# Local attention scores as two-head products two units deep, remote scores by key block, and token transfers that wait for the group in front

## The reference

```
attention: 16 heads, 4 key heads; q = 32 semantic + 32 rotated features, v = 64 features
  keys: 14 means over blocks of 64 tokens (the first 896 tokens) + the last 128 tokens one by one = 142 keys
  scores = (q_sem.k_sem + q_geo.k_geo)/sqrt(32) * exp(logit_scale[h]);  hidden where k_pos > pos
  out = softmax(scores) v, times Wo
  (a token below 63 sees no key: its 142 weights are all equal)
experts: softmax router over 16, the best 4 per token, weights renormed;
  out = sum over the 4 of weight * down_e(silu(gate_e x) * up_e x), inner width 224
```

## Time and profile before

| | us |
|---|---|
| median of the 3 timed runs | 413.79 (413.33 to 415.93) |
| the profiled execution's own time | 414.26 |
| span of its instructions | 412.5 |
| PE busy / DVE busy / ACT busy / POOL busy | 367.9 / 263.2 / 185.9 / 233.3 |
| front (until the first local score) | 0 to 63.7 |
| local stage | 63.7 to 131.2 |
| remote stage | 131.2 to 206.8 |
| expert loop and its tail | 206.8 to 412.5 |

### The profile page before, as it was taken

The page is one execution under the profiler, slowest core; times in us unless marked ns, Lnnn a source line. Parts: engine busy times, 40 slices in busy tenths (PEclk is TensorE's granted clock), DMA queues, the critical chain, the costliest instruction groups (busy, mean ns, idle before and its releaser), DMA issues.

```text
span 412.5 us, 8607 instructions
## 1 busy us (share of the span) xinstructions
PE 367.9 (89%) x2263; PEld 309.1 (75%) x2264; DVE 263.2 (64%) x837; ACT 185.9 (45%) x537; POOL 233.3 (57%) x205
## 2 busy tenths in 40 slices
PE   0599995968998999799899999999999999999991
PEld 0483474756885677577678899999999999999881
DVE  4889244897924799999857755555555555555540
ACT  1541236543521265225537655555555555555550
POOL 3501556566555435994605666566666666666664
PEclk9999997897999999999779999999999999999996
DMA  7991222212114963068545666676667667667544
GB/s 246 357 316 46 78 78 78 78 64 92 52 66 143 319 208 110 21 195 222 152 141 101 104 107 116 103 110 110 111 106 112 114 106 112 112 106 112 78 52 51
DMA packets 49016, 51.41 MB, mean 125 GB/s; under 512 B 5472, under 2 KB 46048, under 8 KB 48992
## 3 DMA queue, kind: packets, MB, share of 16 engines
q0 software_dynamic: 14640, 19.34, 28.3%
q1 hardware_dynamic: 34352, 31.78, 27.2%
HBM read 29.67 MB, written 21.43 MB: 124 GB/s over the span
## 4 chain that ended last, share of the span: by engine, by line
PE 71%; DVE 14%; issue 7%; ACT 3%; DMA 2%; SPq 1%; POOLq 1%; another core or an unknown queue 0%; DVEq 0%; ACTq 0%
PE bank L1292 59%; PE bank L1654 4%; PE bank L1678 4%; DMA x_all<-in_L_attn_x 1%; ACT lex L760 1%; DVE q L1073 1%; DVE q L1070 1%; ACT x_all L692 1%; PE bank L1445 1%; PE bank L1416 1%; DMA out_rows<-y,idx 1%; DVE l L1097 1%; DVE pr L1213 1%; DVE xr L1241 1%; DVE pr L1233 1%
## 5 line engine op out<-in xcount | busy, mean ns | idle before, releaser
L670 POOL DMA_INDIRECT out_rows<-y,idx x79 | 122.9, 1556 | 81.8 <-ACT y L854 63.2
L648 POOL DMA_INDIRECT xn_by_expert<-x_all,slot_i x64 | 64.9, 1014 | 20.4 <-issue 15.7
L1272 DVE SCALAR_TENSOR_TENSOR act<-bank,xg,sg 128x224 f32<-128x224 f32 x79 | 35.6, 450 | 51.5 <-ACT sg L841 50.7
L1292 PE MATMUL bank<-wgu_hi,xh 128*128 x158 | 65.2, 413 | 0.5 <-issue 0.2
L1292 PE MATMUL bank<-wgu_lo,xh 128*128 x158 | 58.5, 370 | 0.0
L1292 PE MATMUL bank<-wgu_hi,xl 128*128 x158 | 57.9, 366 | 0.0
L841 ACT ACTIVATE sg<-bank 128x224 f32<-128x224 f32 x79 | 28.3, 358 | 60.6 <-PE bank L1292 59.7
L1264 DVE TENSOR_TENSOR xl<-bank,xh 128x256 fp32r<-128x256 f32 x79 | 33.5, 424 | 29.4 <-ACT xh L834 29.1
L1292 PE MATMUL bank<-wdn_hi,ah 112*128 x158 | 51.3, 324 | 0.5 <-issue 0.4
L1292 PE MATMUL bank<-wdn_hi,al 112*128 x158 | 44.4, 281 | 0.0
L1292 PE MATMUL bank<-wdn_lo,ah 112*128 x158 | 44.2, 280 | 0.0
(11 more groups left out here) (238 smaller groups left out, 766.1 us busy)
## 6 DMA issues: line engine op xcount, KB each, us to landing
xg<-xn_by_expert SPq DMA_DIRECT2D x79, 129.0 KB, 2.5
wgu<-in_L_ffn_gate_proj SPq DMA_DIRECT2D x16, 224.0 KB, 5.4
wgu<-in_L_ffn_up_proj SPq DMA_DIRECT2D x16, 224.0 KB, 5.8
wdn<-in_L_ffn_down_proj SPq DMA_DIRECT2D x16, 224.0 KB, 6.2
x_all<-in_L_attn_x SPq DMA_DIRECT2D x8, 256.0 KB, 4.8
xr<-in_L_attn_x SPq DMA_DIRECT2D x14, 128.0 KB, 4.6
out_rows<-xr SPq DMA_DIRECT2D x14, 128.0 KB
out_rows<-y,idx POOLq DMA_INDIRECT x79
```

The costliest lines, as they stand in the source:

```text
L648: gp.indirect_dma_start(xs_d, bass.IndirectOffsetOnAxis(slot_i[:, z, r:r + 1], 0), x_all[:, z, :], None).then_inc(xs_in[q], DMA)
L670: gp.indirect_dma_start(out_rows, bass.IndirectOffsetOnAxis(idx[r % RING][:, 0:1], 0), ysb[r % 4][:, :], None, compute_op=ALU.add).then_in ...
L1272: nc.vector.scalar_tensor_tensor(av[t.par][:, :], bank[2 + t.par][:, I:2 * I], xg[t.slot][:, D + 1:D + 2], sg[t.par][:, :], ALU.mult, ALU. ...
L1292: return nc.tensor.matmul(o, lhsT, rhs, start=start, stop=stop)
```

## The change

- **Local scores.** Keys are stored twice per key head with every second head's rows zero (`keep_rep` makes two activations each, scaled by `sscale`). `l_score` makes for each pair of heads one product of 64 rows and 284 columns per feature kind, after a bfloat16 product (identity times mask) that puts the mask into PSUM: 2 + 2 + 2 products into 2 banks. Units alternate between banks (1, 2) and (3, 5), and PE runs two units ahead. DVE's `l_largest` takes minus the maximum straight from PSUM in two reduces; ACT takes the exponentials from PSUM. The copy with the mask is gone.
- **Values.** `fold_values(g)` is one product of 58 weight columns and 512 columns per key head; ACT copies it to `folded`, SP writes it to HBM in the new order (12 DMAs) and reads `vw` back (3 DMAs, semaphore `vw_in`).
- **Columns block by block** (key outer, head inner). Pair t uses 2t+2 blocks, so 32(t+1) columns in scores, exponentials, sums and turns; one turned chunk instead of two for t below 4. The mask of the last two blocks is a bfloat16 product of 32 columns; DVE masks by itself only at t = 0. The maximum is taken from PSUM, and the subtraction reads PSUM and `smax`. PE writes the `bd_g` and `fold_queries` products with four columns together and a step of 16.
- **Token transfers.** Each indirect DMA waits only for the one at the same place p of the group in front.
- **Moved.** `plan_tasks`, `weights(2)`, `weights(3)`, diagonals of `bd_s` go ahead of the local rope, `bound_tasks` behind it; splits: 3 low parts on DVE (was 4), POOL 10 (was 9); experts 13 to 15 are loaded behind the first eight task loads, which the last two stores now part in 4 + 4; their splits come at steps 5 to 7 and 6 to 8, expert 12's high part at step -1.

```diff
-LATE = ((4, 5), (6, 7), (8, 9), (10, 11), (12,), (13, 14, 15))
+LATE = ((4, 5), (6, 7), (8, 9), (10, 11, 12), (13,), (14,), (15,))
-ON_DVE = 4
+ON_DVE = 3
@@ SP
             load_residual(0)
+            for g in range(HKV):
+                sp.wait_ge(fold_kept, g + 1)
+                for m in range(2):
+                    sp.dma_start(vw_rows[:, :, 2 * g + m, :], folded[g % 2][0:FOLD - NB, m, :]).then_inc(folded_out[g % 2], DMA)
+                sp.dma_start(even_rows[:, 2 * g:2 * g + 2, :], folded[g % 2][FOLD - NB:FOLD, :, :]).then_inc(folded_out[g % 2], DMA)
+            for q in range(2):
+                sp.wait_ge(folded_out[q], 3 * HKV // 2 * DMA)
...
+            for i in range(REMOTE - 3):
                 store_sum(i)
                 load_residual(i + 2)
+                if i == 2:
+                    for p in range(GT):
+                        sp.wait_ge(xs_in[p], K * GROUPS * DMA)
+                    load_late(3)
...
+            for j in range(RING // 2, RING):
+                load_task(j, j)
+            for n in range(4, len(LATE)):
+                load_late(n)
@@ POOL
-                    for z in range(q * GT, (q + 1) * GT):
-                        gp.indirect_dma_start(...).then_inc(xs_in[q], DMA)
-                    gp.wait_ge(xs_in[q], (r + 1) * GT * DMA)
+                    for p in range(GT):
+                        z = q * GT + p
+                        if r or q:
+                            gp.wait_ge(xs_in[p], (r * GROUPS + q) * DMA)
+                        gp.indirect_dma_start(...).then_inc(xs_in[p], DMA)
@@ DVE
+                for m in range(2):
+                    last = nc.vector.tensor_reduce(lneg[q][:, 2 * m:2 * m + 2], bank[L_BANKS[q][m]][:, 0:2 * NKEY].rearrange("p (h k) -> p h k", h=2), axis=AX.X, op=ALU.max, negate=True)
...
+                link(nc.vector.tensor_reduce(smax[u][:, :], by_head(scores, t), axis=AX.X, op=ALU.max))
                 if not t.first:
                     dve.wait_ge(c_pt[u], t.count(0))
+                nc.vector.tensor_tensor(by_key(pr[u], t), by_key(scores, t), over_heads(smax[u][:, :], t), ALU.subtract).then_inc(c_d[u], 1)
@@ PE
+                if n >= 2:
+                    pe.wait_ge(l_ex, n - 1)
+                for m in range(2):
+                    mm(out[m], ident_b[:, :], hide_lb[:, :, :].rearrange("p h k -> p (h k)"), True, False)
+                for m, own in enumerate(halves):
+                    mm(out[m], qrT[u][own, g, :], rep_g[own, g, u, :, :].rearrange("p s k -> p (s k)"), False, False)
+                for m, own in enumerate(halves):
+                    last = mm(out[m], qsT[u][own, g, :], rep_s[own, g, u, :, :].rearrange("p s k -> p (s k)"), False, True)
...
+            l_score(0)
+            l_score(1)
+            for n in range(UNITS):
+                l_turn(n)
+                if n + 2 < UNITS:
+                    l_score(n + 2)
+                if n:
+                    l_value(n - 1)
+                beside(n)
+                if n == UNITS - 2:
+                    turn_values(0)
```

More of the change, by code:

```diff
@@ L168, in build @@
         asem = wat.take("asem", [P, NB, DC, HK])
-        vw = wat.take("vw", [HALF + 1, NB, 2, D])
-        bd_g = wat.take("bd_g", [P, NB, HKV, G, NBLK])
-        pr = [wat.take(f"pr{u}", [P, HK + 1]) for u in range(NB)]
+        vw = wat.take("vw", [P, NB, 2, D])
+        bd_g = wat.take("bd_g", [P, NB, HKV, NBLK, G])
+        pr = [wat.take(f"pr{u}", [P, HK]) for u in range(NB)]
         smax = [wat.take(f"smax{u}", [P, H]) for u in range(NB)]
@@ L181, in build @@
         qrT = [wl.take(f"qrT{u}", [P, HKV, P]) for u in range(NB)]
-        prT = [wl.take(f"prT{u}", [HALF + 1, 2, P]) for u in range(NB)]
+        prT = [wl.take(f"prT{u}", [P, 2, P]) for u in range(NB)]
         lpT0 = wl.take("lpT0", [P, G, P])
+        ident_b = wl.take("ident_b", [P, P], BF16)
+        hide_b = wl.take("hide_b", [P, 2, H], BF16)
         wb = r_loop[1]
@@ L431, in first, with keys, cols, chunks @@
                 return self.counts is None and self.off == 0
+            @property
+            def keys(self):
+                return 2 * self.off + 2
+            @property
+            def cols(self):
+                return self.keys * H
+            @property
+            def chunks(self):
+                return [(at, min(P, self.cols - at)) for at in range(0, self.cols, P)]
             @property
@@ L552, in load_residual @@
                         sp.wait_ge(c_stored[u], i * DMA)
-                    sp.dma_start(residual(u, i)[:, :], rows(x_rows, u * TB + i)).then_inc(xr_in[i % 2][u], DMA)
+                    sp.dma_start(residual(u, i)[:, :], rows(x_rows, u * TB + i)).then_inc(lx_in if i == REMOTE - 1 else xr_in[i % 2][u], DMA)
             def store_sum(i):
@@ L574, in _ @@
             load_late(2)
[L575 to L582, removed]
+            load_residual(REMOTE - 1)
+            for i in range(REMOTE - 3):
                 store_sum(i)
                 load_residual(i + 2)
+                if i == 2:
+                    for p in range(GT):
+                        sp.wait_ge(xs_in[p], K * GROUPS * DMA)
+                    load_late(3)
+            store_sum(REMOTE - 3)
             def load_task(j, s):
@@ L592, in _ @@
                 sp.wait_ge(c_s[u], REMOTE)
-            for j in range(RING):
+            for j in range(RING // 2):
                 load_task(j, j)
@@ L837, in step @@
                         p_keep(u, Pair(0, REMOTE - 1))
+                    for k in HEAD:
+                        split_late(k)
                 t = j + 1
@@ L994, in _ @@
             weights(1)
+            weights(2)
             iota_p = const(ca, CA, "iota_p")
@@ L1584, in attend @@
                 o = attended_bank(u, t)[:, 0:D]
-                mm(o, prT[u][0:HALF, 0, :], vw[0:HALF, u, 0, :], True, False)
-                mm(o, prT[u][:, 1, :], vw[:, u, 1, :], False, True).then_inc(c_o[u], 1)
+                parts = [(prT[u][0:rest, n, :], vw[0:rest, u, n, :]) for n, (at, rest) in enumerate(t.chunks)]
+                if t.first:
+                    parts.append((even, vw[0:EVEN_AT + EVENS, u, 1, :]))
+                for n, (turned_p, values) in enumerate(parts):
+                    last = mm(o, turned_p, values, n == 0, n == len(parts) - 1)
+                last.then_inc(c_o[u], 1)
             def attention_pe(t):
```

404 lines of the change are left out of this document (202 added, 202 removed).

## The result

The changed kernel took 467.84 us (median of four, 464.26 to 468.85) against 414.86 for the kernel before on the same chip: a ratio of 1.126, interval 1.118 to 1.134. The forecast was 389, the range 380 to 401. It is slower by 53 us instead of faster by 25.

The account below looks back on a forecast made before the run. PE was taken to lead the local stage, PE and DVE (swollen beside POOL) the remote stage, PE alone the expert loop. Sum: 414.3 - 16.3 (local) - 12.2 (remote) + 3.5 (loop head) = 389.3, so 389 us; range 380 to 401.

Parts of the forecast that it names:

- the one on token transfers: POOL's transfers: about 5.6 us a group instead of 6.91, end at 130 to 138 us, no term in the sum.
- the slower one: Rival, expert loop's head: experts 13 to 15 get only crumbs beside the scatters; 425 us at 35 GB/s, chance 0.03.
- Start of the local stage: Front: stage starts 0.4 us later for the starts product; work moved ahead of it costs nothing.
- Local stage: First score to second `q_project`: 50.8 us instead of 67.5, of which PE's work 46.8; gain 16.3 with the later start.
- A score unit: Local scores: 1.2 us a unit, 0.96 with row halves overlapping plus 0.24 for masks; 2.2 if not.
- The waits: Local stage: 1.6 us at the start and 0.8 of small waits, beside 1.6 for slow clock.
- `vw`: Round trip through HBM in the local stage: back at 35 to 40 us, needed at 42; cover 2 to 7, cost 0.
- Remote stage: Remote pairs: 63.4 us instead of 75.6, with 5.4 less PE work through fewer columns; gain 12.2.
- PE's stalls: Remote stage: 3 us of stalls left of 9.8, between 0 and 9.8, as the subtraction reads PSUM.
- The rival of strided PSUM columns: `bd_g` products and query folds: strided writes slow PE, losing 3 us and 2.7 us; 395 us, chance 0.05.
- Head of the expert loop: Start of the expert loop: costs 3.5 us, as experts 13 to 15 are issued ahead of task 8's load.
- Task 8: Head of the expert loop: its load comes 1 to 8 us late behind the expert loads; 3.5 taken.

Follow-up runs that it names:

- run 9: Changed kernel, not altered, run again as control in another session: 395.61 us, ratio 0.959 to the kernel before.
- run 2: Kernel before, with each token transfer waiting only for the one at its place in the group in front: 410.26 us, ratio 0.993.
- run 11: Changed kernel with one wait a group, remote pairs 1 to 6 taking all 224 columns again (block by block undone): 400.53 us.
- Run 10: Changed kernel with one wait a group, experts 13 to 15 loaded beside remote pair 5, ahead of the task loads: 390.78 us, ratio 0.946.
- first eight runs: Variants of the changed kernel and one of the kernel before (transfer waits, memsets, expert loads), two sessions without late signals: from 391.75 to 415.31 us.
- run 13: Changed kernel, not altered, once more in a further session: 469.12 us.
- run 14: Changed kernel with one single pause in POOL's row of transfers, after the eighth group: 461.35 us.
- run 17: Changed kernel with the wait for the whole group of transfers put back: 418.20 us.
- run 18: Changed kernel with one wait a group and experts 13 to 15 loaded early, in a session with late signals: 460.14 us.
- run 4: Changed kernel with single waits kept and five short memsets on POOL behind each group (7.4 us a group): 407.08 us.
- the best version: Changed kernel with one wait a group and experts 13 to 15 loaded early: 390.78 us without late signals, 460 us with them.
- run 1: Changed kernel with token transfers again waiting for all four of their group: 415.31 us, ratio 1.005.

## Why the prediction was wrong

**The step that failed** is the one on token transfers: "That is no term by itself". The reckoning of the transfers was right (5.3 us a group against 5.6, last one at 127.1 against 130 to 138). What it took away were the group waits, with their pauses and their empty queue, and it asked only who waits for the transfers, not whom they hold up. What the runs showed in its place: PE's signals, and PE itself, were held up until the row of transfers was over, and the local stage started 68.6 us late. The trace of before had a sign. `l` L1097 lists "remote 0.6" in the earlier trace rows, and the waits of ACT hold three more, of which one is this (the kernel before, all engines in order of time):

```profile
85.56 0.66 PE L1445 MATMUL bank<-const_k,lex 128*128 128x128 f32 x4 [0.23 <-issue]
...
86.68 0.97 POOL L648 DMA_INDIRECT xn_by_expert<-x_all,slot_i  x1 [0.30 <-issue]
...
88.57 0.58 ACT L767 COPY lpT<-bank 128x512 f32<-128x512 f32 x1 [1.71 <-remote]
...
89.64 0.19 POOL L645 COPY x_all<-weight 128x4 f32<-128x4 f32 x1 [1.99 <-DMA xn_by_expert<-x_all,slot_i]
```

PE's four turns ended at 86.2, ACT saw it at 88.6, 0.9 us after POOL's last transfer of the group (86.68 + 0.97) and inside its pause. The other three end in a pause of POOL, or as it begins (at 81.78, 102.96 and 109.62). The traces of the sessions without late signals have no such row. A wait of 2 us that nothing in a one-core program ends is a sign that something outside the sum holds signals up. No rival had it either: the slower one was another mechanism at 425.

**The other steps** can be read in the changed kernel's trace without late signals (run 9, span 393.0 us; the forecast as a span is 389.3 - 1.8 = 387.5). Its windows, then PE at the start of the stage:

```profile
65.30:117.20 51.90, 50.62 (x306) 37.06 (x307) 26.90 (x79) 26.28 (x92) 40.28 (x48) 1.00 0.34 118
117.20:179.50 62.30, 60.04 (x336) 42.68 (x334) 53.18 (x125) 27.62 (x63) 41.69 (x29) 1.00 0.57 169
```
```profile
65.32 0.41 PE L1342 MATMUL bank<-hide_lb,ident_b 128*128 128x284 bf16 x2 [0.78 <-ACT qrT L801]
65.66 0.75 PE L1342 MATMUL bank<-rep_g,qrT 64*128 64x284 f32 x4
66.25 0.65 PE L1342 MATMUL bank<-rep_s,qsT 64*128 64x284 f32 x4
66.82 0.42 PE L1342 MATMUL bank<-hide_lb,ident_b 128*128 128x284 bf16 x2
```

- Start of the local stage: 65.3, forecast 64.1 (63.7 + 0.4). 1.2 late: the front was not free. Some 0.7 of it is there at the first copy of `qsT` already (57.45, against 56.71 in run 2, whose front is that of before).
- Local stage: 51.9, forecast 50.8. PE's work is 50.6, not 46.8. A score unit is 1.50 us start to start (66.82 - 65.32), not 1.2: the masks take 0.34 instead of 0.24, the four float32 products 1.16, nearer to full overlap of the halves (0.96) than to none (1.92). That is +2.4 in eight units; the other 1.4 was not taken apart. The waits are 1.3 us and the clock 1.00, where 4.0 had been given for both. Two errors that partly cancel.
- `vw`: SP issues its last loads at 99.6 to 100.9, and PE uses them first at 109.7, without a wait. That is 8.8 us for the landing and the cover. The trace has no landing time for them; with the 2.5 to 5 us of the prediction the cover would be 4 to 6 (an estimate), forecast 2 to 7. 0 was right.
- Remote stage: 62.3 to its last product ahead of the tasks' turns, forecast 63.4. PE's stalls in it are 2.3 (forecast 3.0). The subtraction of 224 columns now takes 0.392 us, beside POOL too, against 1.233 in the earlier trace rows. The product with `srec`, two SBUF inputs, takes 1.145 us for 160 columns beside a split of POOL's (164.2 to 165.4 us), 0.313 for the same 160 columns right behind it, and 0.36 for 192 columns in a gap between two splits (174.3). So far the trace agrees with the Trainium skill ("SBUF — State Buffer", Who interferes with whom), by which two SBUF inputs are blocked and one is not.
- The rival of strided PSUM columns: the four products with `bd_g` of one batch (eight records) take 1.08 us in run 11 at 56 columns, against 0.99 in the earlier trace rows. That is 0.09 a batch, not a slowdown that counts. It doesn't clear the writing itself: the same four take 1.04 us with 8 columns in run 9, so at 56 most of a slower write could still be hidden, as the prediction had said. The sentence in the Trainium skill ("SBUF — State Buffer", the paragraph on cachelines) that any non-contiguous PSUM access pattern slows matmuls significantly is not borne out for these products, in rows of four columns.
- One reading in the prediction is wrong without effect: 0.19 us is the cost of one record of a 224-column product, not of the product (0.76 for four records, which are two products, in the earlier trace rows). The saving was reckoned from the 0.76.
- Head of the expert loop: from the last product ahead of the turns of tasks 0 and 1 to the end 213.5 us (393.0 - 179.5), before 205.7 (412.5 - 206.8), so +7.8 where 3.5 had been forecast. This is the term that was mis-sized.

PE's waits from 200 to 222 us show its parts:

```profile
PE bank L1714 <- DMA xg<-xn_by_expert: 3.9, 1, 3.9
PE bank L1342 <- DVE wdn_lo L1178: 2.5, 1, 2.5
```

Task 8 is 3.9 us late, near the estimate. The 2.5 us are PE waiting for DVE's low part of the last expert. The prediction named these splits, but as waiting for the same bytes as task 8, and put no price of their own on them. Some 1 more are tasks 0 and 1, which wait 1.02 and 0.51 for their rows (before, PE waited 0.57 at that place, for DVE). Run 10, with the loads early, has tasks 8 and 9 in step (200.12 and 202.50, 2.38 apart) and keeps the 2.5. So it isn't the bytes: there ACT has made the last high part by 207.2, and DVE works without a gap until its last low part is done at 210.7. What is left as a cause, and was not tested, is the splits' move to steps 6 to 8 (was 2, 4, 6), for the first gate product of the rolled loop waits for all sixteen low parts, and the kernel before does not stand there.

Together: 1.2 + 1.1 - 1.1 + 4.3 = 5.5, which is 393.0 - 387.5. Without late signals the forecast of 389 stands against 395.6, inside its range, the head of the loop being most of what is missing. In the session of the measurement 67.4 us of later start (132.7 - 65.3) come on top, and 1.1, 2.7 and 1.6 in the stages behind: 72.8 together, the whole difference of the spans (465.8 - 393.0).

## What to carry to other kernels

A wait that goes takes a pause, and a limit on what is under way, with it. Before counting it as waste, look for waits whose releaser the profile doesn't know, and at whether they end in such pauses; in a one-core program a row that says "remote" is a finding, not noise. And when variants disagree with the original, run the original beside them in the same session first: the first eight runs here were read against a time from another one. The same goes within a pair of runs: compare the stretch ahead of the edit's first effect before giving the edit what lies behind it.

## What the runs showed of the hardware

- While GpSimd issued indirect DMAs without a gap (0.97 us each, 0.3 between them), semaphore signals of TensorE reached ScalarE and VectorE up to 52 us after the matmul had ended in the measured trace (58 us in run 13, `vloc`: 63.0 to 120.9), in three of the seven sessions; signals of ScalarE to TensorE were not late (0.14 us). TensorE's own instructions stalled too: eight turns took 4.3 and 17.8 us instead of 1.04. In the other four sessions none was late, in one of them with the same program, whose first twelve transfers start within 0.03 us of the same moments.
- The four timed runs of the changed kernel agreed within each of two sessions (464 to 469 with late signals, 394 to 397 without). How long the single delays are differed by up to 17 us between runs 13 and 14, before their programs differ.
- With a wait for landing after every four transfers (pauses of 1.7 to 2.5 us for most groups) the delays were 3.9 us in all (run 17). In the same session TensorE stood 55.6 us without that wait (run 18).
- While PE stood from 75 to 132 us its granted clock was 0.51, the lower of its two levels (1.2 of 2.4 GHz), and the first score unit behind it ran so: 0.66 us for the mask products that take 0.41 at full clock.
- Open: whether it goes by the chip, what makes the signals late, whether the gap in issuing or the number of transfers under way matters (run 4 in a session with late signals would tell), and whether the best version can be had with pauses short enough to cost nothing. The versions with some 7.4 us a group take 11 to 20 us more than the changed kernel of run 9, with ACT waiting for late expert loads (runs 4 and 1); one between 5.3 and 7 wasn't tried.
